# Scan inputs of a selective-scan block: layernorm coefficients in two parts, and softplus by way of tanh inside the loop

## What is computed

```
h  = layernorm(x)                                  # over the last axis, 128 wide
xc, z = split(h @ W_in.T)                          # 256 and 256 wide
u  = silu(causal_conv1d(xc, conv_w) + conv_b)      # 4 taps along the sequence
dt_raw, B, C = split(u @ W_x.T)                    # 1, 16, 16 wide
dt = clip(softplus(dt_raw @ W_dt.T + b_dt), 1e-4, 10)
A  = -exp(min(A_log, 5))
# then the scan: h = h*exp(dt*A) + dt*B*u; y = h.C
```

## Time and profile before

| | us |
|---|---|
| runs | 1869.15, 1869.20, 1873.27 |
| median | 1869.2 |
| profiled execution | 1870.31 |
| its span (first to last instruction) | 1868.5 |
| scan inputs: load and preparation (1009.94 to 1030.78) | 20.8 |
| scan inputs: loop (1030.78 to 1149.57) | 118.8 |
| scan inputs: softplus after the loop (1149.57 to 1175.52) | 25.9 |

### The profile page before, as it was taken

How to read it: one execution, slowest core, us unless ns; L and a number is a source line. 1 busy time by engine, 2 the same in 40 slices (tenths; PEclk the granted TensorE clock), 3 DMA queues, 4 the chain that set the end, 5 groups by cost and what they waited for, 6 DMA issues and landing times. The chain is left out here.

```text
span 1868.5 us, 36875 instructions
## 1 busy us (share of the span) xinstructions
PE 1580.0 (85%) x10997; PEld 1031.1 (55%) x11024; DVE 1353.5 (72%) x3801; ACT 1034.3 (55%) x2779; POOL 521.2 (28%) x559
## 2 busy tenths in 40 slices
PE   5999999999998999799895885477777774999999
PEld 2666666666665455466563674366655563444444
DVE  4777777777777666577686444799999996677765
ACT  2666666666665333344332225899999992322321
POOL 1211111111111100000000721688888880322200
PEclk9999999999999999899897898798988886999999
DMA  5011011011010900000366000000000001000000
GB/s 136 24 34 34 23 34 34 23 34 34 23 34 5 349 8 0 1 1 1 97 212 183 0 0 0 1 1 0 0 0 0 0 0 51 1 7 6 12 6 17
DMA packets 69336, 66.48 MB, mean 36 GB/s; under 512 B 5695, under 2 KB 66834, under 8 KB 69266
## 3 DMA queue, kind: packets, MB, share of 16 engines
q1 hardware_dynamic: 66598, 64.00, 11.5%
q10 hardware_dynamic: 2668, 1.62, 0.3%
HBM read 61.41 MB, written 4.19 MB: 35 GB/s over the span
## 5 line engine op out<-in xcount | busy, mean ns | idle before, releaser
L1995 PE MATMUL ss_y_ps<-ss_h,ss_diag 128*128 128x256 f32 x1024 | 264.4, 422 | 133.8 <-ACT sc_dt L1913 93.2
L1995 PEld LDWEIGHTS ss_y_ps<-ss_h,ss_diag 128*128 128x128 f32 x1024 | 215.6, 214 | 182.4 <-issue 79.1
L595 ACT ACTIVATE x_probs<-x_probs,x_neg_max 128x257 f32<-128x257 f32 x512 | 253.5, 498 | 63.2 <-DVE x_neg_max L696 63.2
L696 DVE CUSTOM_DVE_ANT_0 x_probs<-x_s_ps,x_mask_b 128x257 f32<-128x257 f32 x512 | 187.3, 423 | 133.5 <-PE x_s_ps L403 133.5
L1897 ACT ACTIVATE ss_decay<-sc_dt,sc_a 128x256 f32 (+1 forms) x496 | 207.8, 479 | 1.8 <-DVE ss_h L1960 1.8
L1951 DVE SCALAR_TENSOR_TENSOR ss_decay<-ss_decay,ss_h 128x1024 f32<-128x1024 f32 x124 | 152.3, 1228 | 27.7 <-ACT ss_decay L1897 27.4
L1907 ACT ACTIVATE ss_come<-ss_dtu,sc_xd 128x256 f32<-128x256 f32 x384 | 163.6, 512 | 6.6 <-POOL ss_dtu L1853 6.6
L413 PE MATMUL x_pT_ps<-all_ident,x_probs 128*128 128x128 f32 x1024 | 162.4, 282 | 0.6 <-DVE x_pT L703 0.6
L1867 POOL TENSOR_TENSOR ss_diag<-all_ident,sc_xd 128x512 f32<-128x512 f32 x128 | 158.8, 1240 | 12.8 <-PE ss_y_ps L1995 2.9
L703 DVE COPY x_pT<-x_pT_ps 128x512 f32<-128x512 f32 x256 | 161.3, 668 | 0.5 <-PE x_pT_ps L413 0.5
L1960 DVE CUSTOM_DVE_ANT_0 ss_h<-ss_come,ss_decay 128x1024 f32<-128x1024 f32 x124 | 149.9, 1209 | 0.0
(11 more groups left out here) (373 smaller groups left out, 3072.0 us busy)
## 6 DMA issues: line engine op xcount, KB each, us to landing
x_ctx_t<-ctxT SPq DMA_DIRECT2D x48, 514.0 KB, 3.8
kept_ctx_t<-ctxT SPq DMA_DIRECT2D x16, 514.0 KB, 8.2
kept_ctx_n<-ctx SPq DMA_DIRECT2D x16, 512.0 KB, 8.5
x_ctx_n<-ctx SPq DMA_DIRECT2D x16, 512.0 KB, 4.1
all_x<-x SPq DMA_DIRECT2D x4, 512.0 KB, 7.8
x_mid<-all_x SPq DMA_DIRECT2D x32, 64.0 KB, 4.0
all_x<-x_mid SPq DMA_DIRECT2D x4, 512.0 KB, 7.6
out<-all_x SPq DMA_DIRECT2D x8, 256.0 KB, 2.0
```

What stands on the lines that cost most here:

```text
L595: ins = nc.scalar.activation(probs[p][:, n, :], probs[p][:, n, :], ACT.Exp, scale=-1.0, bias=neg_max[p][:, n:n + 1], accum_out=sums[p][:, ...
L696: vec.tensor_tensor_reduce(probs[p][:, n, :], s_ps[:, c, 0:S2], mask_b[:, :], -1.0, -MASKED, ALU.add, ALU.min, neg_max[p][:, n:n + 1]).the ...
L1995: ins = nc.tensor.matmul(y_ps[p][:, 0:DI], diag[q][:, m, :], h[q][:, m, :], start=(q == 0 and m == 0), stop=(q == NQ - 1 and m == NH - 1))
```

## The change

Three things are edited. DVE takes the moments of the first quarter alone and makes its coefficients (slice 0 to 8); the moments of the other 24 tiles follow four at a time behind the steps t = -2 to 3, and their coefficients (slice 8 to 32), with their square root on ACT, between steps 3 and 4 (SECOND = 4, MORE = 4). In each step DVE clips dt before the softplus instead of after it, to the bounds whose softplus is 1e-4 and 10, and ACT takes Tanh of Abs(dt)/2 one step behind Abs. After the loop ACT needs only Ln of 0.5 + 0.5 tanh, in four quarters, and DVE one pass a quarter instead of two.

```
+SECOND, MORE = 4, 4
+DT_LOW, DT_HIGH = float(np.log(np.expm1(1e-4))), float(np.log(np.expm1(10.0)))
...
@@ scalar
+                if inside(t - 3):
+                    act.wait_ge(abs_sb, t - 2)
+                    act.sem_inc(waited, 1)
+                    nc.scalar.activation(soft[:, t - 3, :], soft[:, t - 3, :], ACT.Tanh, scale=0.5).then_inc(tanh_sb, 1)
...
-            norm_coefficients(nc, g, act, None, ln_step, lnw)
-            pipeline(act, step, 2, 2, TAPS)
-
-            act.wait_ge(abs_sb, T)
+            first_coefficients(nc, g, act, None, ln_step, lnw, slice(0, QT), 0)
+            for t in range(-2, SECOND):
+                step(t, t % TAPS)
+            first_coefficients(nc, g, act, None, ln_step, lnw, slice(QT, T), 1)
+            for t in range(SECOND, 2 * TAPS):
+                step(t, t % TAPS)
+            with act.Fori(0, T // TAPS - 3) as i:
+                for p in range(TAPS):
+                    step(i * TAPS + (2 * TAPS + p), p)
+            for t in range(T - TAPS, T + 3):
+                step(t, t % TAPS)
+
+            for q in range(LN_Q):
+                t = slice(q * LT, (q + 1) * LT)
+                act.wait_ge(tanh_sb, (q + 1) * LT)
+                nc.scalar.activation(soft[:, t, :], soft[:, t, :], ACT.Ln, scale=0.5, bias=half[:, :]).then_inc(ln_sb, 1)
             act.wait_ge(a_step, 1)
             nc.scalar.activation(a[:, :], a[:, :], ACT.Exp).then_inc(a_step, 1)
-            for half in range(2):
-                quarters = range(half * LN_Q // 2, (half + 1) * LN_Q // 2)
-                for q in quarters:
-                    s = slice(q * LT, (q + 1) * LT)
-                    nc.scalar.activation(soft[:, s, :], soft[:, s, :], ACT.Exp, scale=-1.0).then_inc(exp_sb, 1)
-                for q in quarters:
-                    s = slice(q * LT, (q + 1) * LT)
-                    act.wait_ge(exp_sb, q + 1)
-                    nc.scalar.activation(soft[:, s, :], soft[:, s, :], ACT.Ln, bias=1.0).then_inc(ln_sb, 1)
...
@@ vector
                     vec.scalar_tensor_tensor(dt[:, t - 1, :], w_dt[:, :], xd[:, t - 1, 0:1], b_dt[:, :],
-                                             ALU.mult, ALU.add).then_inc(dt_sb, 1)
-
-            arrived_stats(nc, g, dve, x_in, stats)
-            norm_coefficients(nc, g, None, dve, ln_step, lnw)
+                                             ALU.mult, ALU.add).then_inc(raw_sb, 1)
+                    dve.wait_ge(raw_sb, t)
+                    vec.tensor_scalar(dt[:, t - 1, :], dt[:, t - 1, :], DT_LOW, DT_HIGH, ALU.max, ALU.min).then_inc(dt_sb, 1)
+
+            def moments(tiles):
+                for k in tiles:
+                    dve.wait_ge(x_in[k // QT], 16)
+                    vec.bn_stats(g.bn[:, k, :], g.x[:, k, :]).then_inc(stats, 1)
+
+            moments(range(QT))
+            dve.wait_ge(stats, QT)
+            first_coefficients(nc, g, None, dve, ln_step, lnw, slice(0, QT), 0)
+            step(-3, -3 % TAPS)
...
-            pipeline(dve, step, 3, 1, TAPS)
+            for t in range(-2, SECOND):
+                step(t, t % TAPS)
+                moments(range(QT + (t + 2) * MORE, min(T, QT + (t + 3) * MORE)))
+            dve.wait_ge(stats, T)
+            first_coefficients(nc, g, None, dve, ln_step, lnw, slice(QT, T), 1)
+            for t in range(SECOND, 2 * TAPS):
+                step(t, t % TAPS)
...
-                vec.scalar_tensor_tensor(dt[:, s, :], dt[:, s, :], 0.0, soft[:, s, :], ALU.max, ALU.add).then_inc(soft_sb, 1)
-                dve.wait_ge(soft_sb, q + 1)
-                vec.tensor_scalar(dt[:, s, :], dt[:, s, :], 1e-4, 10.0, ALU.max, ALU.min).then_inc(clip_sb, 1)
+                vec.scalar_tensor_tensor(dt[:, s, :], dt[:, s, :], 0.0, soft[:, s, :], ALU.max, ALU.subtract).then_inc(soft_sb, 1)
```

More of the change, by code:

```diff
@@ L1639, in scan_inputs @@
         soft = sb("soft", [P, T, DI])
+        half = sb("half", [P, 1])
         x_ps, c_ps, u_ps, d_ps = (ps(n, [P, BANK]) for n in ("x_ps", "c_ps", "u_ps", "d_ps"))
@@ L1648, in scan_inputs @@
         waited_pool = sem("waited_pool")
-        waited, abs_sb, exp_sb, ln_sb, soft_sb, clip_sb = (sem(n) for n in ("waited", "abs_sb", "exp_sb", "ln_sb", "soft_sb", "clip_sb"))
+        waited, abs_sb, tanh_sb, ln_sb, soft_sb, raw_sb = (sem(n) for n in ("waited", "abs_sb", "tanh_sb", "ln_sb", "soft_sb", "raw_sb"))
         block = ctx.enter_context(nc.Block())
@@ L1694, in step @@
                     ins.then_inc(xd_psum, 1)
-            pe.wait_ge(prep, TAPS + 2 + 9)
+            pe.wait_ge(prep, TAPS + 3 + 9)
             pipeline(pe, step, 2, 1, TAPS)
@@ L1785, in step @@
                     vec.scalar_tensor_tensor(dt[:, t - 1, :], w_dt[:, :], xd[:, t - 1, 0:1], b_dt[:, :],
-                                             ALU.mult, ALU.add).then_inc(dt_sb, 1)
-            arrived_stats(nc, g, dve, x_in, stats)
-            norm_coefficients(nc, g, None, dve, ln_step, lnw)
+                                             ALU.mult, ALU.add).then_inc(raw_sb, 1)
[9 more added lines that the diff above has]
+            step(-3, -3 % TAPS)
             vec.memset(ones[:, :], 1.0).then_inc(prep, 1)
             vec.memset(cb[:, :], 0.0).then_inc(prep, 1)
+            vec.memset(half[:, :], 0.5).then_inc(prep, 1)
             dve.wait_ge(w_in, 16 * W_LOADS)
@@ L1795, in _ @@
             vec.tensor_scalar(a[:, :], a[:, :], 5.0, None, ALU.min).then_inc(a_step, 1)
-            dve.wait_ge(prep, 2)
-            split_row(vec, dve, prep, TAPS + 2, cb3[:, :], rowmask, (c_hi[:, :], c_rest[:, :], c_f[:, :]), cb[0:3, :])
-            pipeline(dve, step, 3, 1, TAPS)
+            dve.wait_ge(prep, 3)
+            split_row(vec, dve, prep, TAPS + 3, cb3[:, :], rowmask, (c_hi[:, :], c_rest[:, :], c_f[:, :]), cb[0:3, :])
+            for t in range(-2, SECOND):
[5 more added lines that the diff above has]
+                step(t, t % TAPS)
+            with dve.Fori(0, T // TAPS - 3) as i:
+                for p in range(TAPS):
+                    step(i * TAPS + (2 * TAPS + p), p)
+            for t in range(T - TAPS, T + 1):
+                step(t, t % TAPS)
             for q in range(LN_Q):
@@ L1801, in _ @@
                 dve.wait_ge(ln_sb, q + 1)
-                vec.scalar_tensor_tensor(dt[:, s, :], dt[:, s, :], 0.0, soft[:, s, :], ALU.max, ALU.add).then_inc(soft_sb, 1)
-                dve.wait_ge(soft_sb, q + 1)
-                vec.tensor_scalar(dt[:, s, :], dt[:, s, :], 1e-4, 10.0, ALU.max, ALU.min).then_inc(clip_sb, 1)
+                vec.scalar_tensor_tensor(dt[:, s, :], dt[:, s, :], 0.0, soft[:, s, :], ALU.max, ALU.subtract).then_inc(soft_sb, 1)
             dve.wait_ge(a_step, 2)
             vec.tensor_scalar(a[:, :], a[:, :], -1.0, None, ALU.mult).then_inc(a_step, 1)
-            dve.wait_ge(clip_sb, LN_Q)
+            dve.wait_ge(soft_sb, LN_Q)
 def scan_states(nc, g, uz, dt, xd, a):
```

## The result

The changed kernel took 1860.64 us (median of 7 runs, 1858.58 to 1864.48), the kernel before 1870.80 on the same chip (7 runs, 1869.15 to 1873.27): ratio 0.9948, with an interval of 0.9935 to 0.9961. It is 0.5% faster. The profiled execution took 1863.78, with a span of 1861.6; before it was 1868.5.

What follows compares the result with a forecast made beforehand. PE and two ACT instructions bound the loop's step, ACT then DVE the stretch behind, the weights the front. Terms -0.35 + 3.5 + 1.4 - 11.8 - 0.3 = -7.5 gave 1861.7 us, range 1857.5 to 1865.

Steps and rivals of the forecast that it cites:

- First quarter, -0.35: Ahead of the loop: the weights' DMA still holds `w_c`, only `xn` of tile 0 leaves the path, gaining 0.35 us.
- Other moments and clip in steps 0 to 3, 0: In the loop: four moments (0.8 us) and the clip fit in DVE's 1.81 us of idle time, costing nothing.
- The line between `xn` and the long pass: Clip of 256 columns, interpolated between `xn` (128 columns, 0.34 us) and a 2048-column pass (1.23): 0.40.
- Stall, +3.5: Before Silu of tile 5: second coefficients, taking turns with POOL, delay it 3.5 us, between bounds 1.9 and 4.1.
- The rival in which the chain runs free: DVE's six small instructions before the square root aren't held up: stall 1.9, clock stays up, 1858.7 us; chance 0.30.
- Slow spell, +1.4: Behind the stall: PE's clock falls after its gap and PE works slower, costing 1.4 us.
- The bound of 1.66: Slow spell's upper bound: 32 matmuls in the states took 8.83 us behind a 4.36 gap, 7.17 behind 2.59.
- Steps with Tanh, 0: Steps 4 to 31 of the loop: Tanh (0.42 us) fits in ACT's 2.51 idle without a table load, cost 0.
- the growing step: Rival: turns with POOL or Abs waiting for the clip lengthen 28 steps by 0.1 us each: 1864.5 us; chance 0.14.
- the change of tables in every step: Rival: Tanh and Silu need different tables, two loads a step add 15 us over 28 steps: 1877; chance 0.04.
- Behind the loop, -11.8: From last Abs to DVE's last pass: 25.44 us becomes 13.6 with Tanh, one load, Ln and four DVE passes.
- Load at the states, -0.3: The removed 1.28 us load gains only 0.29, as ACT then waits for POOL's `ss_dtu`; bounds 0 and -1.28.

Runs made afterwards that it cites:

- the second series: The changed kernel run once more with no edit, on another chip beside the kernel before: 1862.06 us, ratio 0.9951.

## Why the prediction was right

The forecast was 1861.7 and the median is 1860.64 (1862.06 in the second series), and the time went where the prediction said. That the two lie within 1.1 us is in part luck: the forecast counts from 1869.2, the median of three runs before, where the seven runs have 1870.80; its gain was 7.5, and the medians gained 10.2 in the first series and 7.8 in the second. Term by term, by the changed kernel's profile:

- *First quarter, -0.35*: right in its cause. `w_c` waits for the weights' DMA, and only `xn` left the path; 5.46 became 4.99, so -0.47. (`w_c` came at 1026.22 and not at 1025.3, as the whole stage began 1.20 later.)
- *Other moments and clip in steps 0 to 3, 0*: right. The steps up to Silu of tile 4 grew by nothing that can be seen: from PE's start it is 17.62 us, before 17.78, and that difference goes with the clock, as told below. The line between `xn` and the long pass gave the clip 0.40 with POOL idle; it took 0.29.
- *Stall, +3.5*: 3.84 and 3.64. The choice near the upper bound was right, and for the reason given, turns with POOL: take the products away, and the chain takes 0.98 and the stall is 1.76, close to the lower bound of 1.9. The rival in which the chain runs free is what that kernel shows, and not this one.
- *Slow spell, +1.4*: the term that was most off, 2.23 in the profile shown and 1.48 in the other. The bound of 1.66 came from a single burst; here PE worked at half of the clock for 4.9 us in one execution and 3.3 in another. The step of the prediction that failed is the one from one burst to an upper bound, and the trace of the kernel before shows it already (rows behind this list).
- *Steps with Tanh, 0*: right. From Silu of tile 6 to that of tile 31 it is 89.57 us, before 89.56. ACT loads no table between the one for Silu at 1054.94 and the one for Ln at 1157.39, so both rivals, the growing step and the change of tables in every step, are refuted.
- *Behind the loop, -11.8*: 25.95 became 13.58, -12.37, of which the last Abs gives 0.66 back (its end went from 4.20 to 4.86 behind its Silu): -11.71.
- *Load at the states, -0.3*: -0.15; the small end of the bounds, as argued.

More bursts of the same 32 matmuls in the states, from the trace of the kernel before:

```profile
1301.69 8.74 PE L1995 MATMUL ss_y_ps<-ss_h,ss_diag 128*128 128x256 f32 x32 [2.52 <-ACT sc_dt L1913]
...
1370.40 7.17 PE L1995 MATMUL ss_y_ps<-ss_h,ss_diag 128*128 128x256 f32 x32 [2.52 <-ACT sc_dt L1913]
1381.93 9.56 PE L1995 MATMUL ss_y_ps<-ss_h,ss_diag 128*128 128x256 f32 x32 [4.36 <-ACT sc_dt L1913]
```

Behind gaps of 4.21 to 4.37 there are nine such bursts, with that of the earlier trace rows: seven of 8.83 to 8.86, this one of 9.56 and one of 10.06. They lie 1.66 to 2.89 above 7.17, and the prediction took the lower end of that for its upper bound. And the same gap of 2.52 has a slow burst behind it in one place and a quick one in another, so a gap near 2.59 was no sign either that the clock would hold, as the rival of the free chain has it.

In sum 3.84 + 2.23 - 0.47 - 0.16 (the loop's first steps) - 11.71 - 0.15 is -6.4, and `w_c`, which started 0.33 sooner behind the first weight's DMA (15.08 for 15.41), makes it -6.7; the span fell by 6.9. That these two agree so well is luck again: outside these terms the span has 1.20 us more ahead of the stage and 1.36 less behind the first `ss_dtu`, in code that did not change. The sum was -7.5; the slow spell, 0.8 dearer, and the stall, 0.3 dearer, are the larger part of the difference.

Two figures of the prediction are off in themselves, and its forecast doesn't hang on them: with a drain of 1.4 us its terms make -6.1 and not -6.0, and 24 columns are under a fifth of the 128 of `xn`, not an eighth.

What the prediction didn't look at: equal code takes different times in different executions. Over the ten profiles the time ahead of the stage is 1007.9 to 1012.9 us. The loop's first steps, up to Silu of tile 4, take 17.6 to 18.6, and the granted clock goes with it: from PE's start it stood at half for 7.0 us in the profile shown, 7.8 before, 8.9 in the second profile of the same code and 10.2 with the clip behind the loop, and these steps took 17.62, 17.78, 18.01 and 18.64. That the median gained 10.2 us where the profile gained 6.5 can come from this, for the seven runs lie from 1858.58 to 1864.48 and the one profiled is among the three slowest; what set the others apart isn't shown.

It also priced the first edit as a part of a gain, and the experiments show it as a loss of 5.6 us by the stages inside it: -0.47 at the front against 3.84 + 2.23 in the loop. This was in its sum (-0.35 + 3.5 + 1.4), but only the kernel without the edit tells that nothing of -11.8 depends on it.

## What to carry to other kernels

Before work is moved out of a preparation, look at what ends the wait there: here a DMA did, and 4.8 us of moments that were moved into the loop freed none of it, while one instruction made ahead of the wait gave all there was to have. A short chain on DVE, each link with two inputs, beside a POOL that works without a pause can cost one product of POOL for most of its links (2.8 us for 0.98), so it belongs where POOL is idle, and a stall of PE is to be priced with the half-speed stretch that may follow it. A function of whole-kernel width behind a loop (Exp and Ln by turns, four loads) is worth splitting when one part fits into the idle time of each step.

## What the runs showed of the hardware

- The granted clock after a gap of PE: it stayed up behind 2.20 and 2.58, and fell behind 2.52, 3.62, 4.09 and 4.29. How long PE then worked at half differs too: 3.3 and 4.9 us with the same code, and 6.0 in the profile with the load put back, whose code is the same up to there (gap 4.29, clock at half until 1063.7). Between the states' bursts of the kernel before, one gap of 2.52 was followed by 8.74 us and another by 7.17. The gap's length alone predicts neither, and what does is open.
- At the loop's start, where PE had stood for some 24 us, the granted clock was 0.50 and stayed there for 7.0 to 10.2 us over the ten profiles, while PE worked.
- The edge of a turn: DVE's two-input instructions ended 0.04 to 0.06 us behind the end of POOL's product, and one that began 0.10 us ahead of the next product went first, at 0.19. The same chain took 2.0 and 2.2 us where it began during POOL's copy, and 2.8 where it began during the product behind it.
